# The first heads' operands ahead of the bulk writes, in an attention, MoE and FP4 block

## The reference, cut to what matters

```python
h = _layernorm(x) * (1 + ca) + sa                  # then layernorm again, with gamma and beta: xn
q = (xn @ Wq.T + bq).reshape(b, t, 16, 8)          # k and v in the same way
p = (pos_emb @ Wpos.T).reshape(2 * t - 1, 16, 8)
content_score = einsum('bthd,bshd->bhts', q + u_bias, k)
pos_score = _rel_shift(einsum('bthd,phd->bhtp', q + v_bias, p))
attn = softmax((content_score + pos_score) / sqrt(8))
ctx = einsum('bhts,bshd->bthd', attn, v)
x = x + ga * (ctx @ Wout.T + bout)
```

## Time and profile before

| | us |
|---|---|
| median of three runs | 1046.27 |
| the three runs | 1050.89, 1045.82, 1046.27 |
| profiled execution, its own time | 1040.03 |
| its span, first to last instruction | 1038.1 |
| TensorE busy | 827.2 (80%) |
| VectorE busy | 720.3 (69%) |
| ScalarE busy | 544.9 (52%) |
| GpSimd busy | 390.2 (38%) |

### The profile page before, as it was taken

The page is one execution under the profiler, slowest core; times in us unless marked ns, Lnnn a source line. Parts: engine busy times, 40 slices in busy tenths (PEclk is TensorE's granted clock), DMA queues, the critical chain, the costliest instruction groups (busy, mean ns, idle before and its releaser), DMA issues.

```text
span 1038.1 us, 23774 instructions
## 1 busy us (share of the span) xinstructions
PE 827.2 (80%) x9611; PEld 601.1 (58%) x9611; DVE 720.3 (69%) x1462; ACT 544.9 (52%) x1005; POOL 390.2 (38%) x440
## 2 busy tenths in 40 slices
PE   2483389999999999986379999999998686247774
PEld 1243278888888888865236565666665375125553
DVE  5764655555555555505868988888788588899994
ACT  3880056676667666544555556566564644313332
POOL 3465002434443444334522335234433217313544
PEclk9987589999999999996689999999999799579998
DMA  8048113323333333273000000000000000000111
GB/s 140 6 117 263 49 38 74 83 66 88 91 81 67 90 87 79 60 168 75 0 1 1 2 2 2 1 1 2 1 2 1 1 1 1 0 1 7 21 24 31
DMA packets 55097, 47.37 MB, mean 46 GB/s; under 512 B 22043, under 2 KB 44771, under 8 KB 54243
## 3 DMA queue, kind: packets, MB, share of 16 engines
q1 hardware_dynamic: 36368, 26.43, 10.9%
q0 software_dynamic: 8032, 18.85, 7.1%
q10 hardware_dynamic: 10587, 0.57, 0.7%
HBM read 30.91 MB, written 12.25 MB: 42 GB/s over the span
## 4 chain that ended last, share of the span: by engine, by line
PE 50%; DVE 27%; ACT 6%; POOL 4%; SPq 4%; issue 4%; DMA 3%; POOLq 0%; DVEq 0%; ACTq 0%
PE PS L1102 12%; PE PS L1219 5%; PE PS L1221 5%; PE PS L1220 5%; PE PS L1124 5%; PE PS L1106 5%; PE PS L1081 5%; PE PS L1083 3%; DVE XX L1502 2%; DVE HB L1867 2%; DVE XX L1508 2%; DVE AM L1493 2%; ACT REG L725 1%; DVE ACC L1859 1%; DVE HQ L1996 1%
## 5 line engine op out<-in xcount | busy, mean ns | idle before, releaser
L1621 DVE TENSOR_REDUCE MX<-PS 128x4 f32<-128x1024 f32 x128 | 156.7, 1224 | 119.8 <-PE PS L1083 119.8
L819 ACT ACTIVATE REG<-PS 128x1024 f32<-128x1024 f32 x128 | 130.3, 1019 | 112.9 <-PE PS L1106 107.0
L1102 PE MATMUL PS<-XX,TB 96*128 96x64 f16 x2048 | 159.9, 246 | 2.3 <-DMA XX<-NEG 1.4
L632 POOL TENSOR_TENSOR HH<-HB,HH 128x512 f16<-128x512 f32 x64 | 75.6, 1182 | 172.3 <-ACT HH L870 172.3
L1102 PEld LDWEIGHTS PS<-XX,TB 96*128 96x128 f16 x2048 | 120.6, 119 | 30.6 <-issue 8.0
L900 ACT ACTIVATE SG<-PS 128x512 f32<-128x512 f32 x128 | 76.2, 595 | 110.4 <-PE PS L1221 110.1
L1867 DVE SCALAR_TENSOR_TENSOR HB<-PS,SG 128x512 f32<-128x512 f32 x128 | 87.5, 683 | 44.3 <-ACT SG L900 44.3
L1106 PE MATMUL PS<-XX,KC 97*128 97x128 f16 x1024 | 107.0, 228 | 0.0
L1219 PE MATMUL PS<-XH,XX 128*128 128x512 f16 x256 | 98.5, 385 | 9.9 <-DVE HB L1867 9.7
L1081 PE MATMUL PS<-TM,YY 64*64 64x256 f16 x1024 | 80.8, 332 | 30.5 <-DVE YY L1663 24.3
L1220 PE MATMUL PS<-XH,XX 128*128 128x512 f16 x256 | 97.9, 383 | 0.0
(11 more groups left out here) (236 smaller groups left out, 1717.4 us busy)
## 6 DMA issues: line engine op xcount, KB each, us to landing
REG<-inverse_sums POOLq DMA_DIRECT2D x60, 128.0 KB, 3.0
KC<-keys_strips SPq DMA_DIRECT2D x16, 192.0 KB
keys_strips<-REG POOLq DMA_DIRECT2D x12, 224.0 KB, 8.2
R<-in_L_attn_x SPq DMA_DIRECT2D x32, 64.0 KB, 3.6
XX<-NEG ACTq DMA_DIRECT2D x128, 1.0 KB, 2.1
queries_position<-REG POOLq DMA_DIRECT2D x2, 960.0 KB, 19.0
XX<-queries_position SPq DMA_DIRECT2D x60, 32.0 KB
XX<-queries_content SPq DMA_DIRECT2D x60, 32.0 KB
```

Of the source, the lines that this page charges most:

```text
L819: A(P[jt][:, 1024 * up:1024 * up + 1024].rearrange("p (k x) -> p k x", k=2), ST[u % 2], ACT.Exp).then_inc(exp_done, 1)
L1102: mm(o_pos[:, a], TB[p][0:96, y0:y0 + 128], xp[0:96, 8 * bank + a], start=(a == 0), stop=False, skip_group_check=True)
L1621: nc.vector.tensor_reduce(MX[h % 2][:, :].rearrange("p (r a) -> p r a", r=2)[:, :, 2 * g:2 * g + 2], PS[:, bank:bank + 2, :].rearrange("p ...
```

## The change

The order of the projections becomes six chunks of position queries, the keys, the last two chunks of position queries, the content queries. Their batched copies are made by GpSimd from the high part in SBUF, not by ScalarE from PSUM. VectorE evacuates the last four transposed chunks (semaphore `t_evac_dve`). ScalarE centres the last quarter ahead of projections 2 and 3.

SyncE's list is reordered: strips of the keys first, then the operands of head 0, each behind its own short write, with the load of the position queries and that of the content queries apart; then those of head 1, whose position queries now come from NAT too. GpSimd starts the bulk only when all score operands of head 0 have landed (`x_in[0]`), then makes the wide tiles of head 1 (eight products, `y_wide[1]`), loads head 1's content queries from NAT (`content_first`) and writes the rest. Its fills of XP and XC move from behind the roots to the start of the program. The exponential of block 8 of head 0 also waits for head 1's position queries, since P[1] lies over their source.

The products for the values use the banks 6, 7, 4, 5, 6, 7, 0, 1; maxima of head 0 with odd g use banks 2 and 3. Of the values' evacuations four stand ahead of the maxima of head 0, two between them, two behind. The gates of layer 0 are computed at block 6 of head 0, those of layer 1 at block 11 of head 1. The first burst of head 1 stands behind block 2 of head 0, not block 0.

```diff
-            kind, chunk = (1, c) if c < 4 else (0, c - 4) if c < 12 else (1, c - 8) if c < 16 else (2, c - 16)
-            return kind, chunk, banks[c % 6]
+            kind, chunk = (1, c) if c < 6 else (0, c - 6) if c < 14 else (1, c - 8) if c < 16 else (2, c - 16)
+            return kind, chunk, banks[c if c < 4 else (0, 1, 4, 5, 2, 3)[(c - 4) % 6]]
...
-        X_FIRST, X_LOADS = (16 * (12 + 12 + 2), 16 * (8 + 8 + 2)), 16 * (8 + 8 + 2)
-        Y_LOADS, Y_DENSE = 16 * 3, 16 * 2
+        X_FIRST, X_LOADS = (16 * (12 + 12 + 2), 16 * (12 + 2)), 16 * (8 + 8 + 2)
+        Y_LOADS, Y_DENSE, Y_FIRST = 16 * 3, 16 * 2, (16, 16 * 2)
...
-                slots = [(k, 1, g) for g, k in enumerate((0, 1, 3, 4, 6, 7, 9, 10))]
+                slots = [(k, 1, g) for g, k in enumerate((2, 3, 4, 5, 7, 8, 9, 10))]
...
+        def value_bank(c):
+            return banks[(6, 7, 4, 5, 6, 7, 0, 1)[c]]
...
-            return 6 if h == 0 and g % 2 else 4
+            return 2 if h == 0 and g % 2 else 4
...
+            def first_position_queries(h, strips):
                 p, rows = h % 2, slice(DH * h, DH * h + DH)
-                for j in range(4):
+                for j in strips:
...
+                sp.dma_start(YPD[h % 2], qvb_d[DH * h:DH * h + DH, :].rearrange("d (k x) -> k d x", x=T))\
+                    .then_inc(y_dense[h % 2] if h else position_dense, 16)
+            def dense_content_queries(h):
...
-            sp.wait_ge(high_done, 12)
+            sp.wait_ge(high_done, 14)
             sp.dma_start(khi_d[first, :], NAT[NAT_K][first, :]).then_inc(khi_first, 16)
-            sp.wait_ge(high_done, 16)
-            sp.dma_start(qvb_d[first, :], NQB[first, :]).then_inc(qvb_first, 16)
-            sp.wait_ge(khi_first, 16)
-            maximum_keys(0)
-            sp.wait_ge(stage, 12)
+            sp.wait_ge(stage, 14)
             for h in range(2):
                 for k, part in enumerate((0, 0, 1)):
                     sp.dma_start(k4_d[h, :, k].rearrange("w d x -> d w x"),
                                  NAT[NAT_K + part][DH * h:DH * h + DH, :].rearrange("p (w x) -> p w x", w=4)).then_inc(k_first, 16)
-            sp.wait_ge(qvb_first, 16)
-            sp.wait_ge(qu_first, 16)
-            maximum_stationaries(0)
-            sp.wait_ge(stage, 16)
-            first_position_queries(0)
+            sp.wait_ge(batched, 8)
+            sp.dma_start(qvb_d[first, :], NQB[first, :]).then_inc(qvb_first, 16)
+            sp.wait_ge(khi_first, 16)
+            maximum_keys(0)
             sp.wait_ge(k_first, 16 * 6)
             key_operands(0)
+            sp.wait_ge(qvb_first, 16)
+            dense_position_queries(0)
+            sp.wait_ge(stage, 16)
+            first_position_queries(0, range(2))
+            sp.wait_ge(qu_first, 16)
+            dense_content_queries(0)
+            first_position_queries(0, range(2, 4))
             maximum_keys(1)
-            maximum_stationaries(1)
+            dense_position_queries(1)
+            dense_content_queries(1)
             key_operands(1)
+            sp.wait_ge(y_wide[0], 8)
+            dense_position_queries(2)
+            dense_content_queries(2)
+            first_position_queries(1, range(4))
             sp.wait_ge(max_mm, 8)
             maximum_positions(2)
             maximum_keys(2)
-            maximum_stationaries(2)
-            sp.wait_ge(qv_out, 32)
-            sp.wait_ge(qu_out, 32)
-            score_queries(1)
             for h in range(1, H):
                 if h == 1:
                     sp.wait_ge(khi_out, 16)
                     sp.wait_ge(k_out, 16 * 12)
...
             gp.wait_ge(zeroed, 4)
+            for t in (*XP, *XC):
+                gp.memset(t[:, :].bitcast(F32), 0.0).then_inc(zeroed, 1)
...
                 quarter_root(n, q)
-            for t in (*XP, *XC):
-                gp.memset(t[:, :].bitcast(F32), 0.0).then_inc(zeroed, 1)
             gp.memset(V[:, :], 1.0).then_inc(ones_set, 1)
+            def batched_queries(c):
...
+                chunk = projection(c)[1]
+                gp.wait_ge(high_done, c + 1)
+                for r in range(2):
+                    last = gp.tensor_copy(
+                        NQB[:, 2048 * r + 256 * (7 - chunk):2048 * r + 256 * (8 - chunk)].rearrange("p (w c i) -> p w c i", w=2, c=4),
+                        NAT[NAT_QV][:, 512 * chunk:512 * chunk + 512].rearrange("p (i c w) -> p w c i", c=4, w=4)[:, 2 * r:2 * r + 2])
+                last.then_inc(batched, 1)
+            for c in (*range(6), 14, 15):
+                batched_queries(c)
             rest = slice(FIRST * DH, 128)
-            gp.wait_ge(high_done, 12)
+            gp.wait_ge(x_in[0], X_FIRST[0])
+            gp.wait_ge(khi_first, 16)
+            gp.wait_ge(k_first, 16 * 6)
             gp.dma_start(khi_d[rest, :], NAT[NAT_K][rest, :]).then_inc(khi_out, 16)
-            gp.wait_ge(stage, 12)
             for k, part in enumerate((0, 0, 1)):
                 for w in range(4):
                     gp.dma_start(k4_d[2:H, w, k], NAT[NAT_K + part][2 * DH:128, 1024 * w:1024 * w + 1024]).then_inc(k_out, 16)
-            gp.wait_ge(stage, 24)
             for part in range(2):
-                gp.dma_start(qv_d[1:H, part], NAT[NAT_QV + part][DH:128, :]).then_inc(qv_out, 16)
-            for part, h in ((0, FIRST), (1, 1)):
+                gp.dma_start(qv_d[2:H, part], NAT[NAT_QV + part][2 * DH:128, :]).then_inc(qv_out, 16)
+            gp.wait_ge(y_dense[1], Y_FIRST[1])
+            for j in range(0, 8, 2):
+                own = OWN[:, 8 + j:10 + j].unsqueeze(2).unsqueeze(3).to_broadcast([128, 2, 8, 32])
+                gp.tensor_tensor(YP[1][:, :].rearrange("p (n s a) -> p s n a", n=8, s=8)[:, j:j + 2],
+                                 YPD[1].rearrange("p (n a) -> p n a", n=8).unsqueeze(1).to_broadcast([128, 2, 8, 32]), own, ALU.mult)                    .then_inc(y_wide[1], 1)
+            for j in range(0, 8, 2):
+                gp.tensor_tensor(YC[1][:, :].rearrange("p (n t) -> p n t", n=8)[:, j:j + 2],
+                                 YCD[1].unsqueeze(1).to_broadcast([128, 2, T]),
+                                 OWN[:, j:j + 2].unsqueeze(2).to_broadcast([128, 2, T]), ALU.mult).then_inc(y_wide[1], 1)
+            for w in range(4):
+                for k, part in enumerate(PARTS):
+                    to = 24 * w + 8 * k
+                    gp.dma_start(XC[1][to:to + 8, 1024 * w:1024 * w + 1024],
+                                 NAT[NAT_QU + part][DH:2 * DH, 1024 * w:1024 * w + 1024]).then_inc(content_first, 16)
+            for part, h in ((0, FIRST), (1, 2)):
                 gp.dma_start(qu_d[h:H, part], NAT[NAT_QU + part][DH * h:128, :]).then_inc(qu_out, 16)
             gp.dma_start(qvb_d[rest, :], NQB[rest, :]).then_inc(qvb_out, 16)
...
-                if kind == 1:
-                    for r in range(2):
-                        A(NQB[:, 2048 * r + 256 * (7 - chunk):2048 * r + 256 * (8 - chunk)].rearrange("p (w c i) -> p w c i", w=2, c=4),
-                          bank.rearrange("p (c w i) -> p w c i", c=4, w=4)[:, 2 * r:2 * r + 2], ACT.Identity, bias=VEC3[:, 1:2])
...
-            projected(2)
-            projected(3)
-            transposed_quarter(2)
             centre_quarter(2, 3, HN, h_ready)
-            transposed_quarter(3)
-            for c in range(4, 24):
+            for c in range(2, 24):
...
+                        act.wait_ge(x_in[1], X_FIRST[1])
                     A(P[jt][:, 1024 * up:1024 * up + 1024].rearrange("p (k x) -> p k x", k=2), ST[u % 2], ACT.Exp).then_inc(exp_done, 1)
...
                 pe.wait_ge(h_ready, c + 1)
-                if c >= 2:
+                if c >= 6:
+                    pe.wait_ge(t_evac_dve, c - 5)
+                elif c >= 2:
...
                 kind, chunk, bank = projection(c)
-                if c >= 6:
+                if c in (4, 5):
+                    pe.wait_ge(stage, c - 3)
+                elif c >= 8:
...
-            pe.wait_ge(ld_pos, 16)
-            mm(banks[7][:, 0:NPOS], WPT[:, :], CON[:, C_POS:C_POS + NPOS], start=True, stop=True).then_inc(pe_prep, 1)
-            pe.wait_ge(t_evac, 8)
-            for c in range(4, 24):
+                if q == 1:
+                    pe.wait_ge(ld_pos, 16)
+                    mm(banks[7][:, 0:NPOS], WPT[:, :], CON[:, C_POS:C_POS + NPOS], start=True, stop=True).then_inc(pe_prep, 1)
+            for c in (4, 5):
+                pe.wait_ge(t_evac_dve, c - 3)
                 project(c)
+            pe.wait_ge(t_evac_dve, 4)
+            for c in range(6, 24):
+                project(c)
             pe.wait_ge(prep_done, 4)
             for c in range(8):
-                if c >= 2:
-                    pe.wait_ge(v_done, c - 1)
+                if c in (2, 3):
+                    pe.wait_ge(stage, 20)
+                elif c in (4, 5):
+                    pe.wait_ge(v_done, c - 3)
+                elif c >= 6:
+                    pe.wait_ge(stage, 24)
                 for j in range(4):
```

(58 more changed lines are left out.)

44 lines of the change are left out of this document (21 added, 23 removed).

## The result

The changed kernel takes 1031.4 us in the median of 4 runs (1029.7 to 1033.4), beside 1046.05 for the kernel before: a ratio of 0.986 (95% interval 0.981 to 0.991), 14.6 us less where 23 were forecast. In a later set of 6 runs it took 1028.4 us beside 1043.97 (0.984, 0.980 to 0.988), so the gain is about 15 us. The profiled execution took 1031.96 us, with a span of 1030.1.

What follows compares the result with a forecast made beforehand. Attention is bound by TensorE; ahead lies a hole where head 0 waits for loads behind GpSimd's bulk. Release at 106.0 plus 18.0, 1.0 and 1.5 against 149.86 gives 23.4: 1046.3 - 23 = 1023 us, range 1013 to 1037.

Steps and rivals of the forecast that it cites:

- The last low part: End of the last projection's evacuation before head 0: forecast at 73.9 us against 78.83 before, gain 5 us.
- hole opened at block 12 of head 0: Head 2's maximum operands, loaded beside the second bulk, were to stall block 12 by 1.5 us, bounds 0 and 8.
- rival A: Bulk slows head 1's twelve position loads to 2.9 us each; fifth exponential waits some 14 us; 1037 us; chance 0.20.
- `maximum_scores(0, 0)`: Head 0's first maxima, after operand loads and four widening steps, were to start at 81 to 82 us.
- 106.0. This is the new last wait: Head 1's first maxima were to wait for GpSimd's eight wide products, done at 106.0 us, bounds 101 and 110.
- the anchor: TensorE's first context product, behind block 11 of head 0; at 149.86 us before, forecast 23.4 us sooner.
- 18.0 + 1.0 + 1.5: Way from release to first context product: 18.0 us bursts and low-clock start, 1.0 unhidden layer 0 gates, 1.5 stall.
- the bulk's place behind `x_in[0]`: GpSimd's bulk waits for head 0's operand loads, landed at 88 us, so that head 0 starts earlier.
- B: Whole gain: loads at 0.62 us, no stall at head 2, release at 101.5; gain 30, 1016 us; chance 0.14.
- C: Slower: GpSimd's batched copies ahead of every load at 3 us each cost some 10 us; 1056 us; chance 0.05.
- D: No change: something else fills the hole, which ends near 131 us anyway; 1046 us; chance 0.03.
- the hole: TensorE's idle stretch from 93 to 115 us before head 0's attention, waiting for widened queries behind a late content load.

Runs made afterwards that it cites:

- 1: Changed kernel, but GpSimd makes the products first and starts all bulk only after both halves of head 0's negated maxima landed; 1030.1 us, ratio 0.985.
- 2: Changed kernel, keys' bulk left in place, but query parts, content and batched queries wait until head 0's negated maxima landed; 1021.4 us, ratio 0.978.
- 11: Changed kernel, but only the second bulk (content and batched queries) waits for the second half of head 0's negated maxima; 1026.0 us, ratio 0.982.
- 12: Changed kernel with query parts, content and batched queries held behind the negated maxima, and batched copies back on ScalarE; 1020.7 us, ratio 0.976.
- 4: Changed kernel with the gate taken off keys (stage 14) and query parts (stage 24); content and batched queries still behind the products; 1031.2 us, ratio 0.985.
- 7: Changed kernel with query bulk behind the negated maxima, and SyncE's twelve position loads of head 1 waiting for them too; 1023.3 us, ratio 0.979.
- 3: Changed kernel with the gate taken off the keys' bulk alone, issued at stage 14; query bulk still gated; 1029.9 us, ratio 0.986.
- 5: Changed kernel with the batched query copies back on ScalarE, from PSUM; 1025.8 us, ratio 0.981.
- again: The changed kernel run again, unedited, for a second profile and more times; 1028.4 us, ratio 0.984.
- 9: Changed kernel with query bulk behind the negated maxima and keys' bulk from stage 14, at most two writes in flight; 1026.5 us, ratio 0.982.
- 10: Changed kernel with query bulk behind the negated maxima and keys' bulk from stage 14, one write at a time; 1034.1 us, ratio 0.989.
- 13: Changed kernel with head 1's eight wide products back on VectorE, so GpSimd's second bulk follows its first at once; 1033.6 us, ratio 0.989.

## Why the prediction was right and where it was wrong

**Right.** The last low part ended at 73.31 (forecast 73.9). GpSimd's copies took 0.59 to 0.60 us (0.6), the last at 67.26 (68.2), behind the strip writes. SyncE's six operand loads and ScalarE's twelve went at 0.9 and 0.82 (0.62 and 1.0), and GpSimd's first bulk write stood at 87.22 (88). The steady stretch is as before, and no hole opened at block 12 of head 0, for which the sum had 1.5 us. The time lies in the range, 1013 to 1037, and a gain of 15 us is the lower end of the forecast of 15 to 27. There is luck in that: the wait that cost most wasn't in the sum, and the range held it only because it reached out to rival A.

**Small misses.** `maximum_scores(0, 0)` came at 85.70, not at 81 to 82. VectorE waited for the position queries until 79.15, because I had no price for writing and reading back the batched queries: 4.78 us to land, and then the load. The load of the content queries stood behind that one and six operand loads, was issued at 80.81 (76.0 to 76.6) and landed at 83.04; the two ways ended within 0.2 us of each other. The strip writes took 0.85 each, not 0.6. GpSimd's products took 1.0 each, not 1.18, and ended at 103.9 (106.0), which made up for none of it. TensorE was not released by them, as the forecast had it.

**The step that failed** is "106.0. This is the new last wait". The wait was another one, in a queue that I did not walk: ScalarE's eight DMAs for the negated maxima, which in the kernel before ran from 124.1 us on, when the bulk was gone, at 0.62 us each, and landed in 1.8. The tile `NEG` of the kernel before, 110 to 150 us:

```profile
L773 ACTq DMA_DIRECT2D XX<-NEG x12: 470/617/624, 124.1 to 145.6; - x12
...
DMA to landing us min/median/max: 1.7/1.8/2.2
```

The change puts head 0's maxima at 86 to 98 us, right behind the bulk's start at 87, and these 8 KB meet the 5.57 MB that GpSimd's queue moves from 87 to 111 us. Row four landed at 111.4, block 0 began at 111.55, and head 1's maxima, behind block 2, at 115.48: 9.5 us after the 106.0. From there to the anchor it took 21.95 us where I had 20.5 (18.0 + 1.0 + 1.5); the gates stand in the chain with all of their 2.4 us where I had 1.0, block 4's row adds 2.7, head 2's operands cost nothing where I had 1.5, and the rest of the way took 1.1 less than 18.0. The anchor came at 137.43, not at 126.5, and 12.4 us were gained there in place of 23.4. The experiments that clear the rows' way (1, 2, 11 and 12) show the cause: block 0 comes 17.2, 7.0, 2.0 and 9.0 us sooner. 1 shows which wait stands next.

One more step failed, and 4 shows it: that the bulk's place behind `x_in[0]` shortens the way to the anchor. It does give head 0 an early start (first maxima at 85.70, without it at 102.24), but nothing of it is left at the anchor (137.43, without it 135.85).

**Rival A** had the mechanism and the wrong DMA. It let the bulk bite at head 1's twelve position loads and the fifth exponential. The loads did slow to 2.5 us each and ended at 120.85, but the fifth exponential, at 133.44, was not released by them. In 7 it was, and even there neither the context products nor the time came later. Its 1037 was 6 to 9 us too much. The rule that the Trainium skill gives ("DMA: Bandwidth & Descriptors", Issuing engines are not separate DMA queues), that what the engines issue interleaves, agrees with the rows of negated maxima: 2.1 us to land alone, up to 13.1 beside the bulk. Rivals B, C and D fell: head 1's maxima were released at 115.5, not at 101.5, the copies were as quick as forecast, and the hole ended at 111.6, not at 131.

**The rest of the gap.** The forecast carried the anchor's gain to the end in full; the trace kept 8.0 of 12.4. Laid side by side, VectorE's instructions of the changed kernel run 12.4 us ahead of those of before until 440 us, 10.7 from 590 to 956, and 8.0 at the end. The larger step falls into one stretch of 20 us near the end. The same work in the kernel before, 960 to 980 us, and in the changed one (columns as above):

```profile
960.00:980.00 20.00, 14.46 (x84) 11.29 (x84) 19.28 (x25) 6.89 (x17) 10.97 (x11) 1.00 0.09 19
...
949.20:969.20 20.00, 15.44 (x68) 11.37 (x69) 16.85 (x22) 5.16 (x13) 10.77 (x10) 0.83 0.10 20
```

TensorE's granted clock is 1.00 in the first and 0.83 in the second. "The rest is the same work, shifted" was thus not exact: the same work at a lower clock takes longer. Over the kernels here the distance from the second context product to the end lies between 878.3 and 884.3 us, one execution each (877.9 in the one of before, the shortest of all); the two of the changed kernel have 882.3 and 880.3. The differences come to up to 6 us; what decides them is open. The median gained more than the two profiled executions differ by (14.6 beside 8), because the profiled one of before, at 1040.03, was 6 us below the median.

## What to carry to other kernels

When a bulk of transfers is moved, list every transfer that will be issued or landing in the new place, the smallest ones first: eight writes of 1 KB held this kernel, because each one's landing grew from 2 us to between 8 and 13. Gate a bulk on the last small transfer that the next stage waits for, not on the first, and hold back only the parts whose readers come later: all of it held back was worth nothing over the change (1030.1), the right half of it 10 us (1021.4). When an engine's work comes earlier, walk its own queue for DMAs that it issues. And take each part of a change away by itself before you say what it is worth: the gate that this change was named for was worth nothing (1031.2 without it).

## What the runs showed of the hardware

- A DMA of 1 KB from ScalarE's queue took 0.47 to 0.86 us to issue and 1.9 to 2.9 to land in a quiet stretch, and 0.54 to 3.9 to issue and 7.7 to 13.1 to land beside GpSimd's writes of 224 to 896 KB (DMA share 0.94; 13.9 at most, in the second execution).
- VectorE's negation of 128 x 16 elements took 0.17 to 0.28 us where GpSimd was idle or only issued DMAs, and beside GpSimd's products 0.5 to 1.1 us (experiments 1, 2, 3, 7 and 12), 3.8 (5), 4.0 (again), 4.1 (the change), 4.2 (11) and 8.6 (9); it ended each time at a boundary between two products or behind the last. Reductions from PSUM beside the same products kept their 1.2 us. The Trainium skill ("SBUF — State Buffer", Who interferes with whom) says that GpSimd shares a pair of ports with VectorE as an exclusive lock, and that where a VectorE instruction uses both of its port pairs, whoever issues first has the shared one for the whole instruction and the other is blocked in full. The trace agrees in that the negation is blocked and not slowed in part, and adds that the block can last over several products; in 9 the negation's record even starts first, at 100.81 with the first product at 101.36. In the change it was hidden all but some 1 us: the rows of the first half were being issued until 100.9.
- Waiting for each write of 224 KB on GpSimd's queue costs 3.1 us for one and 4.7 for a pair, where issuing without a wait costs 0.56.
- Projections 4 and 5 of TensorE took 1.88 us in some kernels (1, 5, 9 to 13) and 2.78 to 3.51 in others. The granted clock goes with it: 1.00 throughout in the first, 0.50 for 2 to 3 us in the others. Ahead of them, over 46 to 52 us, TensorE was busy for 2.98 us in the change and 2.94 in experiment 1, at 1.00 in both, so these rows do not say why the clock fell in the one and not in the other.
